# Paged attention in a four-layer stack: own keys grouped by four heads, division moved to the output stage, value pages spread over the partitions, low parts shared out anew

## What is computed

```python
q = rope(rmsnorm(x @ Wq.T)); k = rope(rmsnorm(x @ Wk.T)); v = x @ Wv.T
kc = k_cache[block_table]; vc = v_cache[block_table]      # 512 cached keys
k_all = concat([kc, k]); v_all = concat([vc, v])           # 544 keys, the last 32 are the sequence's own
scores = where(valid, q @ k_all.T * SCALE, -1e30)
probs = softmax(scores)
x = x + (probs @ v_all).reshape(B, S, HQ * D) @ Wo.T
```

## Time and profile before

| | |
|---|---|
| median of 3 runs | 2888.45 us (2887.26 to 2891.68) |
| span of the profiled execution | 2886.1 us |
| attention, first scores to last output matmul | about 1005.7 to 2510.6 us |
| PE busy in the span | 2721.6 us, 94% |
| DVE, ACT, POOL busy | 71%, 50%, 47% |

### The profile page before, as it was taken

One profiled execution on the slowest core, in us unless ns is written; L12 is line 12 of the kernel. 1 busy time (PEld: TensorE's weight loads), 2 busy tenths in 40 slices (PEclk: granted clock), 3 DMA queues, 4 the chain that ended last, 5 costly groups with the idle time before them and its releaser, 6 DMA issues. The chain is left out here.

```text
span 2886.1 us, 58057 instructions
## 1 busy us (share of the span) xinstructions
PE 2721.6 (94%) x16646; PEld 2298.8 (80%) x16647; DVE 2042.3 (71%) x3956; ACT 1441.0 (50%) x2637; POOL 1352.4 (47%) x1008
## 2 busy tenths in 40 slices
PE   7699899999999589999999999999999999799999
PEld 5587677777777478888888888888888888778887
DVE  5355339999999678888888888888888888542221
ACT  3222234444444366666666666666666666431111
POOL 1222165665565555566666666555666666200000
PEclk9899899999999799999999999999999999999999
DMA  6422432332332488887778888888877888353332
GB/s 221 128 76 69 159 109 89 92 102 84 89 89 77 146 248 237 243 237 229 231 237 236 237 234 237 240 236 242 237 229 231 237 236 236 110 208 117 137 109 84
DMA packets 364201, 507.06 MB, mean 176 GB/s; under 512 B 56547, under 2 KB 269731, under 8 KB 360292
## 3 DMA queue, kind: packets, MB, share of 16 engines
q1 hardware_dynamic: 336036, 416.54, 49.2%
q0 software_dynamic: 25984, 86.79, 8.7%
q10 hardware_dynamic: 2112, 2.89, 0.3%
HBM read 407.98 MB, written 98.04 MB: 175 GB/s over the span
## 5 line engine op out<-in xcount | busy, mean ns | idle before, releaser
L1303 POOL TENSOR_TENSOR att_k_lo<-att_k_raw,att_k_hi 128x1024 fp32r<-128x1024 f32 x256 | 606.0, 2367 | 502.4 <-ACT att_k_hi L1337 502.3
L1395 DVE TENSOR_SCALAR att_prob<-att_prob,att_inv_total 128x544 f32<-128x544 f32 x512 | 635.8, 1242 | 0.0
L1329 ACT ACTIVATE att_pt<-att_ps_pt 128x512 f32<-128x512 f32 x512 | 305.8, 597 | 497.6 <-PE att_ps_s L1476 497.6
L1488 PE MATMUL att_ps_o<-att_pt,att_v 128*128 128x128 f32 x4096 | 541.2, 275 | 0.0
L1488 PEld LDWEIGHTS att_ps_o<-att_pt,att_v 128*128 128x128 f32 x4096 | 497.9, 192 | 6.4
L884 POOL TENSOR_TENSOR qkv_part_b<-qkv_normed,qkv_cross 128x256 f32<-128x256 f32 x320 | 297.6, 951 | 240.3 <-DVE qkv_normed L1044 240.3
L1322 ACT ACTIVATE att_prob<-att_prob,att_shift 128x544 f32<-128x544 f32 x512 | 378.4, 739 | 0.0
L76 PE MATMUL att_ps_s<-att_k_hi,att_q_hi 128*128 128x272 f32 x1024 | 349.1, 341 | 26.5 <-POOL att_k_lo L1303 26.1
L1383 DVE CUSTOM_DVE_ANT_0 att_prob<-att_ps_s,att_mask 128x544 f32<-128x544 f32 x512 | 360.2, 704 | 2.2 <-PE att_ps_s L78 2.2
L1473 PE MATMUL att_ps_pt<-att_ident,att_prob 128*128 128x128 f32 x2048 | 318.6, 278 | 23.0 <-DVE att_prob L1395 12.4
L76 PE MATMUL qkv_ps_y<-qkv_w_hi,qkv_xt_hi 128*128 128x512 f32 x768 | 320.2, 417 | 0.0
(11 more groups left out here) (174 smaller groups left out, 4893.5 us busy)
## 6 DMA issues: line engine op xcount, KB each, us to landing
att_k_raw<-in_k_pages SPq DMA_DIRECT2D x1024, 128.0 KB, 3.9
att_v<-in_v_pages SPq DMA_DIRECT2D x1024, 128.0 KB, 3.1
q_t<-qkv_out_t SPq DMA_DIRECT2D x128, 256.0 KB, 2.3
att_q_raw<-q_t POOLq DMA_DIRECT2D x64, 512.0 KB, 4.1
o_t<-att_o POOLq DMA_DIRECT2D x64, 512.0 KB, 6.2
out_o<-o_t SPq DMA_DIRECT2D x32, 1024.0 KB, 6.5
qkv_w_stage<-in_w_qkv SPq DMA_DIRECT2D x12, 1024.0 KB, 5.2
l_w_stage<-in_w SPq DMA_DIRECT2D x8, 1024.0 KB, 7.0
```

What stands on the lines that cost most here:

```text
L1303: pool.tensor_tensor(lo, raw, f32(hi), ALU.subtract).then_inc(pool_split, 1)
L1329: act.activation(pt_sb[:, j % 2, :, :], ps_pt[:, j % 2, :, :], ACT.Copy).then_inc(pt_ready, 1)
L1395: dve.tensor_scalar(prob[:, b, :], prob[:, b, :], inv_total[:, b:b + 1], None, ALU.mult)\
L1488: pe.matmul(out, v_sb[:, p, c, h * DH:(h + 1) * DH], pt_sb[:, j % 2, c, :], start=(c == 0), stop=False)
```

## The change

1. **Own keys at full height.** `gather` on DVE (L1420 of the new kernel) copies a unit's 32 own columns beside those of the three other heads of its group (`p_own`); every fourth unit one 128x128 transpose (L1526) turns all four at once into the spare columns of a score bank. Before it PE waits for the mask of unit u+2. `vo_sb` becomes block-diagonal (zeros elsewhere, loaded by four DMAs of 32 rows each), so that each own matmul (L1544) has 128 rows. `outputs` follows four units behind (`outputs(u-4)`) and stands before `transpose(u)`.
2. **Division in the output stage.** `normalise` and the per-unit reciprocal go. The 8 row sums of a sequence are transposed (L1528), inverted (L1442) and stored (`inv_t`); `output_projection` loads them broadcast over partitions (`load_inv`) and DVE multiplies each half by them (`scale`). `w_stage` has two buffers instead of three.
3. **Spread V pages.** Page n of a value load goes to every fourth partition, from n % 4. Keys keep step with it: high and low parts of a key piece are written with a step of 4 elements (16 bytes), `(k n)` for `(n k)`.
4. **Low parts.** Pieces 2 and 4 stay on POOL; 0, 1, 3 (queries) and 5 go to DVE, at the steps in `LO_AT`; high parts at those in `HI_AT`.

```diff
-PPP, PIECES, PIECE_Q, PIECE_OWN, ON_POOL = 4, 6, 3, 5, 5
-PIECES_AT = [(2,), (3,), (4, 5), (), (), (), (0,), (1,)]
-DVE_PIECES_AT = [(), (), (), (5,), (), (), (), ()]
-EARLY_PIECES = PIECES_AT[6] + PIECES_AT[7]
-LATE_PIECES = sum(PIECES_AT[:EARLY], ())
+HI_AT = [(5,), (2,), (3,), (4,), (), (), (0,), (1,)]
+LO_AT = [(1,), (5,), (), (3,), (), (), (), (0,)]
+EARLY_PIECES = HI_AT[6] + HI_AT[7]
+LATE_PIECES = sum(HI_AT[:EARLY], ())
+ON_POOL = [c for c in PIECE_TURN if c not in sum(LO_AT, ())]
+ON_DVE = [c for c in PIECE_TURN if c not in ON_POOL]
+NB_P = OG
...
-        v_sb, vo_sb = m.sb("v", [P, 2, NPP // 4, HK * DH]), m.sb("vo", [SEQ, 2, HK * DH])
+        v_sb = m.sb("v", [P, 2, NPP // PPP, HK * DH])
+        vo_sb = m.sb("vo", [P, 2, HK // OG, OG, DH])
-        prob = m.sb("prob", [P, 4, NALL])
-        shift, total, inv_total = m.sb("shift", [P, 4]), m.sb("total", [P, 4]), m.sb("inv_total", [P, 4])
-        pt_sb, pto_sb = m.sb("pt", [P, 2, NKEY // P, P]), m.sb("pto", [SEQ, 2, P])
-        o_sb = m.sb("o", [P, 2, HK, P])
+        prob, p_own = m.sb("prob", [P, NB_P, NALL]), m.sb("p_own", [P, 2, OG, SEQ])
+        shift, total = m.sb("shift", [P, NB_P]), m.sb("total", [P, 2, HK])
+        pt_sb, pto_sb = m.sb("pt", [P, OG, NKEY // P, P]), m.sb("pto", [P, 2, P])
+        o_sb, inv_sb = m.sb("o", [P, 2, HK, P]), m.sb("inv", [HK, 2, P])
...
-                    *(b[:, p, :, first * PSIZE:(first + n) * PSIZE].rearrange("p h (n k) -> p n h k", n=n)
+                    *(b[:, p, :, first * PSIZE:(first + n) * PSIZE].rearrange("p h (k n) -> p n h k", n=n)
...
+        def wait_for_lo(eng, s, c):
+
+            if c in ON_POOL:
+                eng.wait_ge(lo_pool, len(ON_POOL) * s + ON_POOL.index(c) + 1)
+            else:
+                eng.wait_ge(lo_dve, len(ON_DVE) * s + ON_DVE.index(c) + 1)
...
+        def spare(half, rows):
+
+            return ps_s[0:rows, 1, half, D - P:D]
...
-                        at = (n % 4) * PSIZE
-                        sp.dma_start(v_sb[at:at + PSIZE, p, n // 4, :], v_pages[bass.ds(page, 1)])\
+                        sp.dma_start(v_sb[n % PPP:P:PPP, p, n // PPP, :], v_pages[bass.ds(page, 1)])\
...
-                    pool.dma_start(vo_sb[:, p, :], v_own[bass.ds(s * SEQ, SEQ), :]).then_inc(own_v_loaded[p], 16)
+                    rows = v_own[bass.ds(s * SEQ, SEQ), :].rearrange("k (g u d) -> k g u d", g=HK // OG, u=OG)
+                    for u in range(OG):
+                        pool.dma_start(vo_sb[u * SEQ:(u + 1) * SEQ, p, :, u, :], rows[:, :, u, :])\
+                            .then_inc(own_v_loaded[p], 16)
...
+                    pool.wait_ge(inv_ready, s + 1)
+                    pool.dma_start(inv_t[bass.ds(s, 1)].rearrange("s (h q) -> (s h) q", h=HK), inv_sb[:, p, :])\
+                        .then_inc(inv_stored[p], 16)
...
+                pool.memset(vo_sb[:, :, :, :, :], 0.0).then_inc(zeroed, 1)
...
+                for c in ON_POOL:
+                    split_lo(0, 0, c)
-                        for c in range(ON_POOL):
-                            raw, hi, lo = piece(c, p)
-                            pool.wait_ge(hi_done, PIECES * s + PIECE_TURN[c])
-                            pool.tensor_tensor(lo, raw, f32(hi), ALU.subtract).then_inc(pool_split, 1)
+                        load_own_v(s, p)
                         if not last:
                             load_q(s + 2, p)
                             load_own_k(s + 2, p)
-                        load_own_v(s, p)
+                        if not (last and p):
+                            for c in ON_POOL:
+                                split_lo(s + 1, 1 - p, c)
                         if later(s, 2):
                             store(s - 2, p)
...
-                    if later(u, 2):
-                        act.wait_ge(pv_done, u - 1)
-                    act.activation(pt_sb[:, j % 2, :, :], ps_pt[:, j % 2, :, :], ACT.Copy).then_inc(pt_ready, 1)
+                    if later(u, OG):
+                        act.wait_ge(pv_done, u - OG + 1)
+                    act.activation(pt_sb[:, j % OG, :, :], ps_pt[:, j % 2, :, :], ACT.Copy).then_inc(pt_ready, 1)
...
-                        copy_pt(u, j)
                         if not (last and j >= UNITS - 2):
                             exponential(u + 2, (j + 2) % UNITS)
+                        copy_pt(u, j)
                         if not (last and j >= EARLY):
                             ahead = j // HK + (2 if j % HK >= EARLY else 1)
-                            for c in PIECES_AT[j % HK]:
+                            for c in HI_AT[j % HK]:
                                 split_hi(2 * i + ahead, i + ahead // 2 + 1, ahead % 2, c)
...
+                def gather(u, j):
+
+                    dve.wait_ge(exp_done, u + 1)
+                    dve.tensor_copy(p_own[:, j // OG % 2, j % OG, :], prob[:, j % NB_P, NKEY:NALL]).then_inc(gathered, 1)
...
-                def invert(u, j):
-                    dve.wait_ge(exp_done, u + 1)
-                def normalise(u, j):
-                    b = j % 4
-                    dve.wait_ge(inverted, u + 1)
-                    dve.tensor_scalar(prob[:, b, :], prob[:, b, :], inv_total[:, b:b + 1], None, ALU.mult)\
-                def copy_own(u, j):
-                    dve.wait_ge(t_done, u + 1)
-                    if later(u, 2):
-                        dve.wait_ge(pv_done, u - 1)
-                    dve.tensor_copy(pto_sb[:, j % 2, :], ps_s[0:SEQ, (j + 1) % 2, 1, D - P:D]).then_inc(pto_ready, 1)
+                def copy_own(i, g):
+                    dve.wait_ge(t_done, UNITS * i + OG * (g + 1))
+                    if later(i, 1) or g >= 2:
+                        dve.wait_ge(pv_done, UNITS * i + OG * (g - 1))
+                    dve.tensor_copy(pto_sb[:, g % 2, :], spare(1, P)).then_inc(pto_ready, 1)
+
+                def invert(i, p):
+                    dve.wait_ge(t_done, UNITS * i + HK * (p + 1))
+                    if later(i, 1):
+                        dve.wait_ge(inv_stored[p], 16 * i)
+                    dve.reciprocal(inv_sb[:, p, :], spare(0, HK)).then_inc(inv_ready, 1)
...
+                        if j % OG == 0 and later(u, OG):
+                            copy_own(*group_before(i, j, 1))
+                            if j % HK == 0:
+                                invert(*group_before(i, j, 1)[:1], (1 - p))
                         if not (last and j >= UNITS - 2):
                             wait_for_scores(2 * i + (j + 2) // HK, u + 2, (j + 2) % UNITS)
                         if not (last and j >= UNITS - 1):
-                            invert(u + 1, j + 1)
+                            gather(u + 1, (j + 1) % UNITS)
...
-                        copy_own(u, j)
-                        if not (last and j >= UNITS - 1):
-                            normalise(u + 1, j + 1)
+                        if not (last and j >= HK - 1):
+                            ahead = 2 if j % HK == HK - 1 else 1
+                            for c in LO_AT[j % HK]:
+                                split_lo(s + ahead, (p + ahead) % 2, c)
+                        if j % OG == 1 and later(u, 2 * OG):
+                            copy_o(*group_before(i, j, 2))
...
-                        pe.wait_ge(pool_split, ON_POOL * (2 * i + p + 1))
-                        pe.wait_ge(dve_split, (PIECES - ON_POOL) * (2 * i + p + 1))
+                        wait_for_lo(pe, 2 * i + p, ON_DVE[-1])
+                        wait_for_lo(pe, 2 * i + p, ON_POOL[-1])
-                    if later(u, 3):
-                        pe.wait_ge(pto_ready, u - 2)
+                    if j % OG == 3 and later(u, OG + 3):
+                        pe.wait_ge(pto_ready, UNITS // OG * i + j // OG)
+                    if h == 3 and later(u, HK + 3):
+                        pe.wait_ge(inv_ready, 2 * i + p)
...
-                    pe.wait_ge(normed, u + 1)
+                    pe.wait_ge(exp_done, u + 1)
...
-                    pe.transpose(ps_s[0:SEQ, (j + 1) % 2, 1, D - P:D], prob[:, j % 4, NKEY:NALL], ident[:, :])\
-                      .then_inc(t_done, 1)
+                        mm = pe.transpose(ps_pt[:, j % 2, c, :], prob[:, j % NB_P, c * P:(c + 1) * P], ident[:, :])
+                    if j % OG == OG - 1:
+
+                        if not (last and j == UNITS - 1):
+                            pe.wait_ge(masked, u + 3)
+                        pe.wait_ge(gathered, u + 1)
+                        mm = pe.transpose(spare(1, P), p_own[:, g % 2, :, :].rearrange("p u k -> p (u k)"), ident[:, :])
+                    if j % HK == HK - 1:
+                        mm = pe.transpose(spare(0, HK), total[:, p, :], ident[:, :])
+                    mm.then_inc(t_done, 1)
...
-                    if h == 0:
-                        pe.wait_ge(own_v_loaded[p], 16 * (i + 1))
-                    pe.wait_ge(pto_ready, u + 1)
-                    pe.matmul(out, vo_sb[:, p, h * DH:(h + 1) * DH], pto_sb[:, j % 2, :],
```

(34 more changed lines are left out.)

108 lines of the change are left out of this document (56 added, 52 removed).

## The result

The changed kernel takes 3070.97 us (median of 4 runs, 3067.22 to 3072.95), the kernel before 2889.25 beside it: a ratio of 1.0626, 95% interval 1.0611 to 1.0641. It is slower by 182 us where the forecast was 182 faster. The profiled execution spans 3070.0 us; SP's first issue of the output stage, 2516.20 before, is at 2676.92, so 161 us were lost by the end of attention and 23 in the output stage.

A forecast was written before the change was run, and what follows sets the result against it. The prediction took PE, busy 94% of the span, as the bound. Attention's -203 us, +5 at its ends and +16 in the output stage gave -182, so 2706 us; its own range was 2660 to 2772.

The forecast's parts named there:

- Strided key pieces: Attention's key pieces written with a 16-byte step: priced as contiguous, 1.05 us on ACT and 2.37 on POOL.
- signs that the prediction had named for its being wrong: In attention, strided ACT, DVE or POOL pieces lasting over 1.05, 1.2 and 2.4 us would refute the forecast.
- The doubled case: Attention's strided key pieces at twice the contiguous price: 4.91, 1.91 and 2.29 us by the 128x2048 rows.
- the slower rival: Attention's strided pieces cost double: 26.2 us a sequence, 3094 us in all; chance 0.10 for double or near it.
- PE's work: Attention on PE, waiting for nothing: 2.36 us a unit instead of 2.81, 18.85 a sequence.
- The own passes: PE's own matmuls in attention: 0.112 us each, like value passes; with these, 0.98 + 0.42 becomes 1.12, saving 0.28.
- the turn back from 32 rows: Attention's slow first product after the own passes: if this turn causes it, 0.10 us a unit goes.
- Gather behind POOL: Attention: DVE's gather waits for POOL's low part, delaying the mask; PE waits 0.5 us at the own transpose.
- Store of the inverted sums: Attention: DVE's `invert` waits some 1.5 us for this store's landing; 0.8 of it reaches PE.
- Waits in all: PE's two waits in attention together: 1.3 us a sequence, between 0 and 2.2, making a sequence 20.15.
- Output stage: Second tile starts 56.3 us after SP's first issue instead of 40.0: 16 us more, 24 with landings of 7.8.
- The no-waits rival: Attention's waits absorbed: SP's 19.28 us a sequence gives 2651, or PE's 18.85 gives 2623; chance 0.18.

The follow-up runs named there:

- e1: Changed kernel with part 3 undone (key pieces contiguous, V pages on neighbouring partitions, keys in natural order): 2709.51 us.
- e2: Changed kernel with ACT's high parts alone written without a step, DVE and POOL keeping it: 2889.42 us.
- e3: Changed kernel with the low parts on DVE and POOL read and written without a step, ACT keeping it: 2911.28 us.
- e9: Changed kernel, strided pieces and spread V pages kept, with POOL's two low parts a sequence made by DVE: 2965.3 us.
- e4: e1 with the V pages spread again, a page on every fourth partition, key pieces still contiguous: 2801.98 us.
- e10: Changed kernel with each V page on 32 neighbouring partitions again, key pieces keeping their 16-byte step: 3070.69 us.
- e7: e1 with POOL's two low parts a sequence made by DVE, POOL only issuing DMAs: 2653.11 us.
- e6: Kernel before the change with part 3 alone added (16-byte key step, spread V pages): 2957.17 us.
- e11: e7 with half of each V page left out, the same number of transfers: 2654.35 us.
- e8: e7 with four of a sequence's sixteen V pages issued by POOL in place of SP: 2684.36 us.

## Why the prediction was wrong

**The step that failed is "Strided key pieces".** It took 1.05 us for ACT and 2.37 for POOL from the nearest contiguous rows, and the change's 1.2 on DVE. Measured: 2.06, 2.88 and 2.05, all three of them signs that the prediction had named for its being wrong. In their place the runs showed 361 us for part 3 in this order (e1), which come back by about half when either ACT's step or the low parts' goes (e2, e3).

The doubled case stood there as the far end and as the slower rival: 26.2 us a sequence and 3094 us, at a chance of 0.10. It came out at 25.8 and 3071. Its path, a late high part on ACT, POOL's low part late, the gather and the mask behind them and PE waiting for that mask, is in the trace, but that its number is so near is luck. POOL's low part was 2.88 us and not 4.9, under the 3.8 that the rival held to be needed with ACT unchanged. DVE's own low parts, which it didn't price, nearly doubled; and with no low part on POOL the kernel still takes 2965 (e9). And it had no term for the clock, some 1.5 us a sequence.

**A second price was missing in the same step.** The spread V pages were costed at nothing without a word on SP's issuing. With them a sequence takes 21.6 us in e4, where SP's queue waits for nothing, against 20.0 in e1; that is 92 us. It didn't move the result (e10), as SP wasn't the bound; had the pieces been free, it would have been 2802 and not 2706.

**The rest of the sum held in total, with terms that were off against each other.** With part 3 undone it gives 2709.5 against 2706:
- PE's work: 18.85 us a sequence forecast, 18.8 measured (e7), and 2.36 a unit against 2.31 to 2.32 for one without an own transpose. The own passes are 0.11 apart, as forecast. The first product still takes 0.21, so the 0.10 wasn't the turn back from 32 rows; the four transposes take 0.36 and not 0.44, which makes up for it.
- Gather behind POOL: 0.5 us a sequence forecast at the own transpose, 0.75 measured (44.1 us in 59 waits, e1, to the end of attention); e7 shows the cause by removing it.
- Store of the inverted sums: 1.5 us forecast, of which 0.8 was to reach PE; almost nothing measured. In e1 `invert` waits for it twice in 64 times, 1.0 us in all. The store of the output lands in 4.9 us and that of the sums in 5.0, near the 5.3 taken, so the instants I gave for the chain ahead were too late.
- Waits in all: 1.3 forecast, 1.2 to 1.3 measured (20.0 less 18.8). That this agrees is luck: the second wait isn't there, the first is longer, and in e1's timeline two units without a recorded wait are 0.18 and 0.10 us longer than the 2.31 of the others.
- Up to the output stage's first issue: 201 us less in e1, 198 forecast.
- Output stage: 16 us forecast, 21.6 in e1 (391.5 us from SP's first issue to the end, 369.9 before). The first product is in time (the terms as listed add up to 16.5 and not 16.7, which changes nothing); the pairs of weight groups are later by 4 until the second tile, with landings of 6.5 to 6.7 us (medians of the changed kernel) where 5 was taken.
- The no-waits rival: 2651 by SP's 19.28 us a sequence. e7, where PE's waits for the mask are gone, takes 2653 at 19.2 a sequence. PE's 18.8 is close below, so SP and PE bound it nearly together.

## What to carry to other kernels

A step in an access pattern is an operand's price on every instruction that touches it, here on eight of the ten large ones in a sequence. Where no row has it, two instructions on the chip with and without the step are worth more than any nearest row. Price each edit in what its engine stands ahead of: part 3 cost 67 us in the old order and 361 in the new one, which also gives DVE some of the dearer low parts. When no engine is full and the span is longer all the same, look for short operations with a long mean, such as a copy of 32 columns at 0.58 us here, or a low part of 128x256 at 3.12 in e6: both stood beside a low part on POOL.

## What the runs showed of the hardware

- fp32 on 128x1024: a step of 16 bytes makes ACT's copy (strided writes) 2.06 us instead of 1.05, DVE's subtraction (one strided read, strided write) 2.05 instead of 1.22, POOL's 2.88 instead of 2.37. ACT's row shows that strided writes alone are dear; for DVE and POOL no run parts the read from the write. A step of 8 bytes: 1.15, 1.22, 2.42. The Trainium skill's "GPSIMD Engine Reference", section "Performance pitfalls for Q7 kernels", gives half as much again for reads with a step over 8 bytes in code for POOL's cores; in this subtraction, with one of two reads and the write strided, it was 22%.
- Beside a low part on POOL, DVE's copy of 128x32 took up to 2.26 us (0.17 with no low part there, e7), and its subtraction on 128x256 took 3.12 instead of 0.41 (e6).
- A 128 KB page onto every fourth partition takes SP 0.63 us to issue (16 in 10.05), onto neighbouring ones 0.46 to 0.53.
- After an idle time of 3.15 us PE ran at a granted clock of 0.54 for 3.3 us.
- A reciprocal of 8x128 takes 0.93 us on DVE, more than the mask of 128x544 with 0.71.
- A DMA share of 1.00 (288 GB/s) was not yet a bound: a fifth fewer bytes brought it to 0.75 and left the time (e7, e11). With a second queue that issued pages beside SP's (e8), SP's key issues took 0.7 us instead of 0.5 and the landings of key pages 6.7 us instead of 3.3 (e7).
